# Attention on one core: the three bf16 parts of q and k taken out of PSUM by TensorE, and half of the causal masks made by GpSimd

## What is computed

```python
qkv = target @ w_qkv                                   # (16, 256, 384)
q, k, v = jnp.split(qkv, 3, axis=-1)                   # each to 16 heads of 8
scores = jnp.einsum('bhqd,bhkd->bhqk', q, k) * (1.0 / np.sqrt(HD))
scores = scores * causal - (1.0 - causal) * NEG
attn = jax.nn.softmax(scores, axis=-1)
out = jnp.einsum('bhqk,bhkd->bhqd', attn, v)
...
x = _layernorm(x + _layernorm(out @ w_proj + b_proj + x) * gamma + beta)
x = _layernorm(x + experts(x))                         # top 2 of 14, weighted
```

## Time and profile before

| what | value |
|---|---|
| time, median of 3 executions | 470.4 us (468.29 to 470.57) |
| the profiled execution | 471.32 us |
| its span, first to last instruction | 469.6 us |
| mean granted TensorE clock | 0.931 of full speed |
| busy: PE, DVE, ACT, POOL | 78%, 68%, 59%, 54% of the span |
| attention stage (to the last scatter) | about 0 to 314 us |
| a step in the steady part | 15.43 us |

### The profile page before, as it was taken

One profiled execution on the slowest core, in us unless ns is written; L12 is line 12 of the kernel. 1 busy time (PEld: TensorE's weight loads), 2 busy tenths in 40 slices (PEclk: granted clock), 3 DMA queues, 4 the chain that ended last, 5 costly groups with the idle time before them and its releaser, 6 DMA issues. The chain is left out here.

```text
span 469.6 us, 13082 instructions
## 1 busy us (share of the span) xinstructions
PE 364.5 (78%) x4355; PEld 268.6 (57%) x4355; DVE 317.6 (68%) x1001; ACT 276.6 (59%) x672; POOL 254.9 (54%) x341
## 2 busy tenths in 40 slices
PE   3648999887898989898889786307999888984940
PEld 2325566555566656665556454207988877871940
DVE  7355568978588898889888854354777666750591
ACT  2203666666477667767776485206999888840074
POOL 5600043545346654665455467641777777774382
PEclk9999999999799999999999899556999999998895
DMA  3521247864323323333230010033333333311742
GB/s 100 151 62 48 61 117 192 228 134 104 88 72 106 93 77 87 98 92 91 63 84 25 25 43 30 23 108 74 103 97 103 99 94 101 98 47 54 249 147 89
DMA packets 72254, 44.09 MB, mean 94 GB/s; under 512 B 12641, under 2 KB 67955, under 8 KB 72076
## 3 DMA queue, kind: packets, MB, share of 16 engines
q1 hardware_dynamic: 64856, 32.70, 26.5%
q0 software_dynamic: 4672, 9.36, 6.0%
q10 hardware_dynamic: 2660, 1.20, 1.0%
HBM read 18.61 MB, written 12.43 MB: 66 GB/s over the span
## 5 line engine op out<-in xcount | busy, mean ns | idle before, releaser
L909 DVE TENSOR_REDUCE row_max<-M 128x4 f32<-128x1024 f32 (+1 forms) x96 | 117.1, 1219 | 35.0 <-PE M L1192 34.2
L705 ACT ACTIVATE probs<-S 128x768 f32<-128x768 f32 x128 | 102.6, 817 | 52.9 <-PE S L1159 51.1
L670 POOL DMA_INDIRECT results<-tile_rows x78 | 79.9, 1024 | 35.7 <-issue 20.9
L635 POOL DMA_INDIRECT sorted_rows<-x,row_no x64 | 65.0, 1015 | 41.2 <-DVE row_no L967 27.9
L1097 DVE COPY probs<-experts 128x642 f32 x78 | 47.8, 613 | 24.8 <-DVE tile_rows L1106 22.5
L1186 PE MATMUL M<-k_stack,q_stack 64*128 64x128 bf16 (+1 forms) x512 | 40.8, 262 | 29.9 <-DVE row_max L909 28.9
L1375 PE MATMUL M<-probs,hT 128*128 128x128 f32 x312 | 52.1, 291 | 9.0 <-DVE tile_rows L1106 5.8
L1210 PE MATMUL O<-probs,diag 128*32 128x256 f32 (+1 forms) x1024 | 56.6, 341 | 0.5 <-DVE row_chosen L948 0.5
L792 ACT ACTIVATE hT<-S,probs 128x128 f32<-128x128 f32 x156 | 49.0, 364 | 2.5 <-PE S L1368 1.4
L1375 PEld LDWEIGHTS M<-probs,hT 128*128 128x128 f32 x312 | 41.4, 194 | 15.9 <-ACT hT L792 8.0
L1368 PE MATMUL S<-rows_t,probs 128*128 128x128 f32 x312 | 49.6, 283 | 0.3 <-ACT rows_t L786 0.3
(11 more groups left out here) (193 smaller groups left out, 709.2 us busy)
## 6 DMA issues: line engine op xcount, KB each, us to landing
q_stack<-diag SPq DMA_DIRECT2D x96, 64.0 KB
tile_rows<-sorted_rows SPq DMA_DIRECT2D x78, 64.5 KB, 1.9
k_stack<-diag SPq DMA_DIRECT2D x78, 64.0 KB
xin<-in_L_attn_target_dram SPq DMA_DIRECT2D x16, 128.0 KB, 2.5
xres<-in_L_attn_target_dram SPq DMA_DIRECT2D x16, 128.0 KB, 2.5
q_stack<-results SPq DMA_DIRECT2D x8, 256.0 KB, 3.1
k_stack<-results SPq DMA_DIRECT2D x8, 256.0 KB, 3.7
out_dram<-probs SPq DMA_DIRECT2D x8, 256.0 KB, 2.3
```

Of the source, the lines that this page charges most:

```text
L635: pool.indirect_dma_start(sorted_rows, bass.IndirectOffsetOnAxis(ap=row_no[:, q * 2 * TT + n:q * 2 * TT + n + 1], axis=0), x2[:, q, n % 2, ...
L670: pool.indirect_dma_start(results, bass.IndirectOffsetOnAxis(ap=y_rows[:, slot, D:ROW].bitcast(U32), axis=0), y_rows[:, slot, 0:D], None, ...
L705: act.activation(probs[:, n].rearrange("p (a q) -> p a q", a=2), S[n % 2][:, :].rearrange("p (a q) -> p a q", a=2)[:, :, 0:T + P], ACT.Exp ...
L909: dve.tensor_reduce(row_max[:, (r - 2) % R, :, g0:g0 + ng, half], M_both[:, :].rearrange("p (a h k) -> p a h k", a=2, h=ng), X, ALU.max).t ...
```

## The change

GpSimd makes a second constant, `minus_ident`, the negated identity in bf16. The tile `rest`, DVE's `split` and POOL's subtraction are gone. `project` leaves its matmuls open to accumulation; after ACT's cast to `part_h`, PE adds `minus_ident` times `part_h` to G (`take`, one matmul of 128x512), so that G holds what is left; ACT casts G to `part_m`, PE takes that away too, and ACT casts G to `part_l`. G is now free only when `part_l` is cast: the waits on `rest_left` for G become waits on `l_split`. In the steady steps the first `take` stands at the end of u = 2 and the second at the end of u = 3, each with a wait on ACT's cast; ACT's third cast stands in u = 3 behind its copy of the heads.

For units 3 to 6 of each sequence `scores` leaves out the four mask matmuls. POOL sets the upper triangle of `probs` to zero after the exponential instead, with two `affine_select` instructions of 128x2x128 for each unit, and `values` waits on `masked`.

```diff
+        minus_ident = sb("minus_ident", [P, P], BF16)
-        rest = sb("rest", [P, 2, T])
...
+        SELECTED = (3, 4, 5, 6)
...
+                    s, n = s_unit(t, u)
+                    if on(s) and n in SELECTED:
+                        pool.wait_ge(exp_done, NP * s + n + 1)
+
+                        for at in (0, T):
+                            diag = probs[:, n, :].rearrange("p (a q) -> p a q", a=2)[:, :, at:at + P]
+                            last = pool.affine_select(out=diag, in_=diag, compare_op=ALU.is_ge, fill=0.0, base=0,
+                                                      pattern=[[0, 2], [1, P]], channel_multiplier=-1)
+                        last.then_inc(masked, 1)
                     if u == 6 and on(t - 4):
                         after(pool, ys_done, t - 4)
...
-                    if u == (0 if early(t) else 3) and on(t):
-
-                        if t >= R:
-                            pool.wait_ge(stacked[r], stack_count(t - R))
-                        pool.wait_ge(m_split, t + 1)
-                        pool.tensor_tensor(part_l[:, r], rest[:, :, :], part_m[:, r], ALU.subtract).then_inc(l_split, 1)
...
                         act.wait_ge(rest_left, t + 1)
-                        act.copy(part_m[:, r], rest[:, :, :]).then_inc(m_split, 1)
+                        act.copy(part_m[:, r], G[:, :].rearrange("p (w q) -> p w q", w=2)).then_inc(m_split, 1)
                     if u == 0 and on(t) and early(t):
+                        act.wait_ge(last_left, t + 1)
+                        act.copy(part_l[:, r], G[:, :].rearrange("p (w q) -> p w q", w=2)).then_inc(l_split, 1)
...
+                    if u == 3 and on(t) and not early(t):
+                        act.wait_ge(last_left, t + 1)
+                        act.copy(part_l[:, r], G[:, :].rearrange("p (w q) -> p w q", w=2)).then_inc(l_split, 1)
...
-            def split(t, r):
-
-                dve.wait_ge(h_split, t + 1)
-
-                after(dve, l_split, t)
-                dve.tensor_tensor(rest[:, :, :], G[:, :].rearrange("p (w q) -> p w q", w=2), part_h[:, r],
-                                  ALU.subtract).then_inc(rest_left, 1)
...
+                if n not in SELECTED:
...
             def values(t, r, s, k):
+                after(pe, masked, len(SELECTED) * s + len([n for n in SELECTED if n <= 2 * k + 1]))
...
                 elif on(t - 1):
-                    pe.wait_ge(rest_left, t)
+                    pe.wait_ge(l_split, t)
...
-                    last = pe.matmul(G[:, w * T:w * T + T], wqk[:, w], xT[:, r], start=True, stop=True)
+                    last = pe.matmul(G[:, w * T:w * T + T], wqk[:, w], xT[:, r], start=(w == 0), stop=True, skip_group_check=True)
...
+            def take(part, r, sem):
+
+
+                pe.matmul(G[:, :], minus_ident[:, :], part[:, r].rearrange("p w q -> p (w q)"), start=False, stop=True,
+                          skip_group_check=True).then_inc(sem, 1)
...
+                        for part, split, left in ((part_h, h_split, rest_left), (part_m, m_split, last_left)):
+                            pe.wait_ge(split, t + 1)
+                            take(part, r, left)
...
                         if on(t):
-                            pe.wait_ge(rest_left, t + 1)
+                            pe.wait_ge(l_split, t + 1)
...
+                    if u == 2 and on(t) and not early(t):
+                        pe.wait_ge(h_split, t + 1)
+                        take(part_h, r, rest_left)
+                    if u == 3 and on(t) and not early(t):
+                        pe.wait_ge(m_split, t + 1)
+                        take(part_m, r, last_left)
```

More of the change, by code:

```diff
@@ L279, in transformer_layer @@
         exp_done = sem("exp_done")
+        masked = sem("masked")
         pv_done = sem("pv_done")
@@ L896, in body @@
                             dve.memset(zeroed(q_stack[:, i]), 0).then_inc(queries_zeroed[i], 1)
-                    split(t, r)
+                    if t == 0:
+                        masks_below()
                     if t < 2:
@@ L977, in body @@
                     last.then_inc(ys_done, 1)
-                if on(t) and not early(t):
-                    split(t, r)
                 reduce(3)
@@ L1154, in scores @@
                                          q_stack[rows, b, n, T - nq:T], start=(half == 0), stop=True, skip_group_check=True)
[L1155 to L1160 removed]
+                if n not in SELECTED:
+                    for c in range(2):
+                        for a in range(2):
+                            rows = slice(TILE * a, TILE * a + TILE)
+                            diag = S[n % 2][:, 512 * a:512 * a + 2 * T].rearrange("p (k q) -> p k q", k=2)[:, :, TILE * c:TILE * c + TILE]
+                            last = pe.matmul(diag, mask_s[rows, c], ident_fold[rows, None, :].broadcast_to([TILE, 2, TILE]), start=False,
+                                             stop=True, skip_group_check=True)
                 last.then_inc(s_ready, 1)
```

12 lines of the change are left out of this document (3 added, 9 removed).

## The result

The changed kernel takes 480.33 us (median of 4 runs, 479.22 to 481.92) against 469.35 of the kernel before (468.26 to 470.57); the ratio is 1.023, 95% interval 1.020 to 1.026. It is slower, and the time lies 1.1 us from the forecast. The profiled execution took 480.34 us with a span of 478.6, 9.0 more than that of before, which was itself 2 us above its median.

A forecast was written before the change was run, and what follows sets the result against it. No engine was full; in steady steps PE and DVE take turns. Terms 4.4 + 0 + 2.0 + 0.5 + 1.9 = +8.8 us on the profiled 471.32 gave 480.1, less 0.9 to the median: 479.2 us, range 472.0 to 484.5.

The forecast's parts named there:

- The start: Steps 0 to 2: casts and takes in one chain delay the first reduction, +4.4 us, bounds 3.6 and 5.0.
- Wrong altogether if the first reduction comes before 22: Sign at the start: first reduction forecast at 25.2 instead of 20.84; before 22 would refute the forecast.
- Steps 3 to 7: Attention steps after the start: no net change, 0 us, bounds -0.7 and +0.5.
- The reduction followed PE: Steps 3 and 4: the reduction in question waited on PE, not on `rest`; part of the 0 us term.
- The steady steps: Steps 8 to 15: 0.45 us gain outweighed by `chosen` colliding with `x_beta`; +0.25 us a step, +2.0 in all.
- rival 2: Steady steps: no hold-up of small DVE instructions, and L1014 escapes the scatter; step gains up to 0.9, 467.7 us; chance 0.06.
- set by SP's queue: Steps 6 and 7: SP's DMA queue, not compute, sets their time; part of the 0 us term.
- Steps 16 and 17: Steps without new x, takes or `rest`: the same collision, +0.25 us each, +0.5 in all (-0.6 to +1).
- The last steps: From step 18: selects delay POOL's chain that ACT waits for, +1.9 us, bounds 0.8 and 2.6.
- Rival 1: Steady steps through 17: small DVE instructions not held up, ten steps at -0.45 us, 472.4 us; chance 0.20.
- Rival 3: POOL's selects: twice as slow, 0.9 us each, so POOL bounds the step; 490 us; chance 0.08.
- Rival 4: Start: the split costs only 1 us instead of 4.4, as values or third cast find a gap; 476 us; chance 0.13.

The follow-up runs named there:

- b_minus_late: a_pool_pause with the negated identity made behind the folded masks; 519.38 us on a chip where the kernel before took 531.89.
- a_pool_pause: Changed kernel with GpSimd again waiting for `m_split` in each of steps 0 to 2; 476.84 us, ratio 1.015 to the kernel before.
- a_takes_only: Changed kernel with all score masks on TensorE again and no selects, takes and three casts kept; 487.38 us, ratio 1.040 to the kernel before.
- c_xbeta: Changed kernel with `x_beta` made at the end of unit 3 instead of behind unit 4's selects; 478.77 us, ratio 1.017 to the kernel before.
- a_early_old: Changed kernel with sequences 0 to 2 split the old way, without takes there; 469.62 us, ratio 1.002 to the kernel before.
- d_no_selects: c_combo with all masks on TensorE, no selects, and the fourth scatter waiting for the shift; 467.94 us, ratio 0.996 to the kernel before.
- c_combo: Changed kernel with old split for sequences 0 to 2, late `minus_ident`, early `x_beta`, selects for sequences 0 to 13 only; 465.01 us, ratio 0.988 to before.
- a_masks_only: Kernel before plus only the selects, the wait on `masked` and the missing mask matmuls; 468.98 us, ratio 1.000 to the kernel before.
- b_masks_xbeta: Kernel before plus selects for sequences 0 to 13 and `x_beta` at the end of unit 3; 517.66 us beside 531.89 for the kernel before.
- b_xbeta: Changed kernel with `x_beta` made at the end of unit 3, same program as c_xbeta; 522.71 us beside 531.89 for the kernel before.

## Why the prediction was right, and where only its total was

**The start, +4.4, measured +11.75.** Casts and takes in one chain were near: 5.15 us by b_minus_late, just above the upper bound of 5.0. The take and the second period came as written; the first period was reckoned too short (it is 6.95, with the gate's transpose in it) and so was the last stretch (5.02 us from the third projection to the maxima, 4.4 reckoned). ACT's chain had been misread: its rounds start 5.50 and 5.45 us apart before (8.67, 14.17, 19.62), not 5.02, and 7.01 and 6.97 after (15.27, 22.28, 29.25), not 6.6; so the third take of `part_h` waits 1.12 us for ACT, 0.4 more than the others. The step that failed is one that was never made: of `part_l` only its 1.16 us were taken off POOL, not its wait for `m_split`, which at the start had kept GpSimd's memsets apart from VectorE's constants (4.65 us, a_pool_pause). Nor did the 0.56 us of `minus_ident` stand in any term; its place cost another 1.94 us (b_minus_late), and without it the copies might not have met the memsets at all. "Wrong altogether if the first reduction comes before 22" looked to the wrong side.

**Steps 3 to 7, 0, measured -3.2.** In step 3 it is -1.34: the pieces of maxima take 0.60 to 0.64 us up to 46.92 and 0.39 from 51.88 on before, 0.61 up to 51.76 and 0.39 from 54.12 on after, so that the last three pieces of step 3 are slow ones before and fast ones after. The granted clock is 1.00 in all four stretches; on the two speeds see the last section. In steps 4 to 7 it is -0.30 to -0.58 each. "The reduction followed PE" was true, and for that reason the masks taken off PE count there, and were left out: a_takes_only, which keeps them, gives back 0.57 us in steps 4 and 5 where the changed kernel gives 0.88. In steps 6 and 7 L1014's hold-up goes as well (0.81 and 0.63 to 0.19).

**The steady steps, +0.25 each, measured -0.06.** The mechanism was right and its size was not: c_xbeta, which frees `chosen`, falls by 0.34 us a step, to 0.40 below the step of before. So the undisturbed gain came nearly as reckoned (0.45), and the hold-up of `chosen`, reckoned at 0.70 (from -0.45 to +0.25), cost half of that. From the start of `chosen` to that of the reduction it is 1.05 us before, 1.30 after and 0.94 in c_xbeta; the forecast had 1.67 (179.73 to 181.4). `x_beta` starts 0.18 us ahead of `chosen` and not 0.08, and from its end to the reduction it is 0.76 us and not 1.03: `both` and the statistics were taken too long.

L1014's 0.63 us, kept as they were in the forecast, became 0.19. That was rival 2's condition, which had been argued away with the gate matmul, where the pair of selects ahead of the scatter was the thing to count. But it brought little: from the start of the shift to that of the choice of experts (MAX8) it is 1.73 us instead of 1.84, 0.11 for the 0.44 of the rival. In c_xbeta, where neither instruction is held up as before, the step gains 0.40 and not rival 2's 0.9.

In steps 8 and 9 another 1.1 us were given back, around the wait for the shift's DMA (timeline of PE, counterpart of the earlier trace rows):

```profile
127.17 0.34 PE L1156 MATMUL S<-q_stack,k_stack 64*128 64x256 bf16 x4 [2.47 <-DMA q_stack<-shift_t]
```

It is 0.91 us shorter than before. That is not a late start being swallowed: a_early_old, 1.5 us early at the shift of sequence 5, waits 2.44 us there and gains 1.4 in these two steps, while a_pool_pause, 4.0 us late, waits 2.70 and gains nothing. So "set by SP's queue" does not hold as it was written, and what sets this wait stays open.

**Steps 16 and 17, +0.5, measured +0.2**: +1.0 in one and -0.8 in the other. **The last steps, +1.9, measured +1.7.** a_takes_only, without selects, loses 0.3 there, so 1.4 us are the selects. d_no_selects and c_combo lose 1.0 and 1.2 there though sequences 14 and 15 have no selects in them; what they share is the early `x_beta`. c_xbeta, with both, loses 3.8.

**Rivals.** Rival 1 fell (`chosen` was held up). Rival 2's steps of 14.6 us did not come. Rival 3 fell (0.41 us a select). Rival 4 fell the other way. Two sums are off: ten steps at -0.45 are -4.5 and not -4.3, which makes rival 1 472.2 us, and the lower bounds of the terms add up to -0.5 us, some 470 and not 475.

The terms were off by +7.3, -3.2, -3.5, -0.3 and -0.2 us, which makes +0.1 together. The total is right because errors cancelled; its sign rests on the start, which the forecast and rivals 1 to 4 all had as a loss.

c_combo shows what the change can be worth when its side effects are removed, with `x_beta` moved besides. The takes cost 5 us where one sequence after another is split. From sequence 3 on, takes, ordering wait and early `x_beta` together make the step 0.17 us shorter than before (d_no_selects); none of the three was run alone on the kernel before, so their shares are not shown. The selects pay 0.23 us a step on TensorE (d_no_selects against c_combo), and the rest of what they seemed to pay was the order in which they put GpSimd's work.

## What to carry to other kernels

When a diff deletes an instruction, list the waits that go with it, and ask what the engine behind it will now do earlier and beside whom; when it adds one ahead of others, ask what it pushes into whose way. On GpSimd that neighbour matters more than its own time: a wait that orders its work, and one instruction moved into a gap (d_no_selects), were worth 0.9 us in each step, four times what the removed matmuls were. And a total that comes out right is tested by its terms: mark the same event in both traces at each stage and take the differences.

## What the runs showed of the hardware

**VectorE behind GpSimd, with one operand too.** The prediction reckoned with instructions of two SBUF operands. The rows above show a copy of bf16 (5.85 us for two, 0.64 before), a `tensor_scalar` (0.82 to 2.57 for two) and the copy of `place` (0.16 to 0.60) held up as well, while memsets on VectorE (0.91 us) and reductions from PSUM (1.19 to 1.23) kept their time throughout. The Trainium skill names copies and `tensor_scalar` among those that can contend (SBUF — State Buffer, "Who interferes with whom"); only the half on two inputs had been used. By that section of the Trainium skill the loser waits for the other's whole instruction. The rows show more than one: a single copy took 5.377 us, from 6.45 to 11.83, and GpSimd's three memsets of the stacks and the one of `diag`, which ran without a gap from 6.46 to 11.79, lie in that time.

Beside a scatter it depends on the moment. In all the traces the second instruction of the shift (L1014) took 0.19 to 0.25 us where it started up to 0.25 us behind the start of a scatter, and 0.62 to 0.81 where it started 0.32 to 0.51 behind it. It is no rule for others: `ys`, which started 0.39 us behind the scatter at 170.25, was not held up. What makes the difference stays open.

**One form at two speeds.** The prediction took a piece of maxima at 0.61 us for the start and at 0.39 for later, with a granted clock of 1.00 in both. The trace of d_no_selects shows it otherwise. Timeline of PE, and windows:

```profile
26.34 0.61 PE L1205 MATMUL M<-k_stack,q_stack 64*128 64x256 bf16 x4 [1.33 <-DVE row_max L928]
```

```profile
24.00:39.00 15.00, 9.15 (x74) 5.78 (x75) 8.06 (x9) 1.44 (x3) 3.27 (x4) 0.50 0.16 44
```

Here the pieces take 0.39 us at 17.64 and at 22.14 (for which TensorE had waited 4.01 us), 0.61 from 23.97 to 36.44, and 0.39 to 0.40 from 39.69 on, and the granted clock is 0.99 from 17.0 to 22.6, 0.50 (the 1.2 GHz level) from 24 to 39 and 1.00 from 40 on. In a_masks_only the slow pieces at 43.89 and 46.09 lie in a stretch of 0.61. So in these two traces the slow form goes with the lower level. In those of before and after the granted clock reads 1.00 beside the slow form too, and no run shows why.

**A stall that belongs to one chip.** In the four traces of the second session VectorE stood once a step in front of the same reduction, the fourth behind a shift, in six to nine steps of the attention stage: for 1.6 to 2.2 us in three kernels and 1.4 to 1.5 in b_masks_xbeta. In b_xbeta TensorE's maxima were done at 182.02 in the step shown. Timeline of DVE:

```profile
184.02 1.22 DVE L914 TENSOR_REDUCE row_max<-M 128x4 f32<-128x1024 f32 x1 [2.05 <-remote]
```

The profile names no engine for it ("remote"). In c_xbeta, the same kernel on another chip, the same reduction starts at 178.06 without a wait. That step was 16.74 us there and 15.05 here. What VectorE waited for stays open; it was not tried.
